# Loading image 0 once: its 32 partitions on ScalarE's queue, the gate's products on them in place

## The chip, the cores and the metric

One core of a Trainium2 chip. The metric is device time in microseconds (us) of one execution; the time before is the median of three runs. Durations below come from one profiled execution of the same program, and times of rows count from the start of its span.

## The reference, cut to what matters

`x` has 32 images of 96 channels, 56 x 56, fp32. Two steps follow each other on it. Cut down:

```python
# step 1: a gate on image 0 picks one of 32 filters for each channel
g    = relu(bn2(einsum('nchw,oc->nohw', x, wg1))).mean(axis=(2, 3))
xg0  = (relu(tanh(g @ wg2.T + bg2)) + beta)[0]
p    = round(xg0[:31] / xg0.sum() * 96)             # the bounds between the filters
filt = ...                                          # (96, 7, 7), chosen by the bounds
xp   = x.reshape(n, 96, 7, 8, 7, 8).mean(axis=(3, 5))
y    = relu(bn1(sum(xp * filt) @ w1d[:, :, 1].T + b1d))
x    = x * (1 + y)
# step 2: a depthwise 3x3 convolution whose taps are made from the image itself
t    = relu(norm(x.mean(axis=(2, 3)) @ w1.T))
wt   = (t @ w2.T + b2) masked to four taps: upper left, up, upper right, left
out  = depthwise_conv(x, wt) + bias
```

Of the gate only image 0 counts, yet the filters of every image hang on it.

## The kernel before, in words

The work is cut into 8 groups of 4 images. A group has 3 tiles of 128 partitions (4 images x 32 rows of channels; channel 3q + t of an image is in tile t), each with 3136 fp32 a partition: 1568 KB. There are 24 tiles, 9 input buffers (`xin`) and 4 output buffers (`xout`). Image 0 is the partitions 0 to 31 of the tiles 0, 1 and 2.

Order of the work: the order in the program of each engine is written by hand, and semaphores join the engines.

- **The gate.** Image 0 is loaded a second time, ahead of the tiles, by three DMAs of 392 KB on SyncE's queue (L338 and L339) into the last output buffer: each row of 3136 pixels is spread as four quarters over four partitions, so that 128 partitions are used. The gate's weights come by a fourfold broadcast (L335) into `gate_one`; VectorE spreads them over a 128 x 128 block `gate_w` (L467), and TensorE makes six matmuls of 128 x 392 (L812), t = 0, 1, 2 by two halves, with two warm products (L779, on zeros) ahead of t = 2. ScalarE takes relu with a sum (L686) and tanh (L689); VectorE and TensorE assign a filter to each channel (L575 to L595), and L833 makes the filters by partition.
- **The cell sums.** Each tile needs its 49 sums of 8 x 8 cells. Tiles 0 to 2 are summed by TensorE (L786, with an identity matrix), VectorE (L504) and GpSimd (L406 folds, VectorE then reduces, L519). Later tiles are folded by GpSimd and reduced by VectorE ahead of their turn: `AHEAD` is 5, and the fold of tile k + 6 stands in GpSimd's program after the edge columns of tile k (L447). The sums of tile 3 (L504 again) stand between the steps that make the coefficients of group 0, and the sum of tile 4 stands in tile 0's turn, after its first tap (L637).
- **The coefficients.** L541 weighs the cells of a group, small matmuls (L841 to L862) with ScalarE and VectorE between them make four taps for each channel and image, and L571 writes them into `coef`.
- **The convolution.** For each tile the output rows are shared: the first 15 by VectorE (L637), 27 by TensorE with VectorE finishing (L871, L647), 14 by TensorE with ScalarE finishing (L880, L738). TensorE uses diagonal matrices of 64 x 64 made by ScalarE (L711); ScalarE seeds banks (L715). L871 works on own rows into own columns, L880 on own rows into the other half's columns.
- **Queues.** SyncE's program issues, in this order: the gate's weights, identity (L337), image 0, the tiles 0, 1, 2 (tile 2 in two parts), the wide constants (L359), tiles 3 to 8, and then, as buffers come free, the load of tile k + 9 (L366 to L368) and the store of tile k (L375). The last tiles' stores are partly crossed (L352): two stores of 64 partitions each. ScalarE's queue carries two small loads: early (the other gate and normalization constants, L679) and narrow (L680).

Of the kernel before, what the change touches and what calls it, by code (L numbers as in the profile page):

```python
# [6 lines left out]
NIMG, C, H, W = 32, 96, 56, 56  # L7
HW = H * W
P = 128
QUAD = 32  # L10
PER = C // QUAD
GROUP = P // QUAD
# [3 lines left out]
BLK = H // DCT  # L16
CELLS = DCT * DCT
NF = 32
# [6 lines left out]
PAD = W  # L25
BANK = 512

IN_BUFS = 9
OUT_BUFS = 4
# [18 lines left out]
QUARTER = HW // 4  # L48
# [5 lines left out]
HEAD_PART = 5  # L54
# [4 lines left out]
E_GATE2 = E_GATE1 + NF  # L59
# [3 lines left out]
E_END = E_HID + 4  # L63
# [11 lines left out]

W_QUARTER = 0
W_IDENT = W_QUARTER + GROUP
W_BIAS = W_IDENT + P
# [48 lines left out]
def build(nc, x, early, narrow, wide, out):  # L127
    fp32 = mybir.dt.float32
    ALU = mybir.AluOpType
# [3 lines left out]
    x_tiles = x.rearrange("n c h w -> (n c) (h w)").rearrange("(g p t) f -> g t p f", p=P, t=PER)  # L133
    out_tiles = out.rearrange("n c h w -> (n c) (h w)").rearrange("(g p t) f -> g t p f", p=P, t=PER)
    x_image0 = x[0, :, :, :].rearrange("c h w -> c (h w)").rearrange("(q t) (j f) -> t q j f", t=PER, j=GROUP)

    with ExitStack() as ctx:
        def sb(name, shape):
            return ctx.enter_context(nc.sbuf_tensor(name, shape, fp32))

        def sem(name):
            return ctx.enter_context(nc.semaphore(name))


        xin = sb("xin", [P, IN_BUFS, PAD + HW])
        xout = sb("xout", [P, OUT_BUFS, HW])
        halves = sb("halves", [P, 2, DCT, BLK * W // 2])
        gate_one = sb("gate_one", [P, PER * E_END])
        gate_w = sb("gate_w", [P, PER, P])
        gate_in = sb("gate_in", [P, E_HID - E_GATE2])  # L150
# [49 lines left out]
        w_hid = wide_sb[0:C, W_HIDE:W_IMAGE]  # L200
        quarter_of = wide_sb[:, W_QUARTER:W_IDENT]
        ident = wide_sb[:, W_IDENT:W_BIAS]
# [3 lines left out]
        to_rows = wide_sb[0:C, W_SPREAD:W_EYE].rearrange("p (t r) -> p t r", t=PER)  # L206
        image0 = xout[:, OUT_BUFS - 1, 0:PER * QUARTER].rearrange("p (t f) -> p t f", t=PER)

# [69 lines left out]
        zeroed = sem("zeroed")  # L278
        gate_placed = sem("gate_placed")
        pad_zeroed = sem("pad_zeroed")  # L280
# [53 lines left out]
        def _(sp):  # L334
            sp.dma_start(gate_one[:, :], early.rearrange("(q j t) e -> q j (t e)", j=1, t=PER).broadcast_to(  # L335
                [QUAD, GROUP, PER * E_END])).then_inc(gate_one_in, 16)
            sp.dma_start(wide_sb[:, 0:W_BIAS], wide[:, 0:W_BIAS]).then_inc(ident_in, 16)  # L337
            for t in range(PER):  # L338
                sp.dma_start(image0[:, t, :], x_image0[t]).then_inc(image0_in[t], 16)  # L339

            def load(k, first=0, end=H):
                return sp.dma_start(xin[:, k % IN_BUFS, PAD + first * W:PAD + end * W],
                                    x_tiles[k // PER, k % PER][:, first * W:end * W])

# [9 lines left out]

            load(0).then_inc(loaded[0], 16)
            load(1).then_inc(loaded[1], 16)
            load(2, 0, HEAD_PART * BLK).then_inc(part_in, 16)
            load(2, HEAD_PART * BLK, H).then_inc(loaded[2], 16)
            sp.dma_start(wide_sb[:, W_BIAS:W_END], wide[:, W_BIAS:W_END]).then_inc(wide_in, 16)  # L359
# [34 lines left out]
        def _(pool):  # L394
# [18 lines left out]

            for j in range(2):
                pool.wait_ge(loaded[j], 16)
                fold_once(j, *FOLDED)
# [5 lines left out]
            def diagonals(k):  # L422
# [6 lines left out]
                                  each.broadcast_to([P, TAPS, HALF]), ALU.mult).then_inc(tail_diag_done, 1)  # L429

            for k in range(TILES):
                if k + 1 < TILES and crossed(k + 1):
# [26 lines left out]
        def _(dve):  # L459
            vec = nc.vector  # L460
            vec.memset(zeros[:, :], 0.0).then_inc(zeroed, 1)
            vec.memset(xin[:, :, 0:PAD], 0.0).then_inc(pad_zeroed, 1)

            dve.wait_ge(gate_one_in, 16)
            dve.wait_ge(ident_in, 16)
            for t in range(PER):
                vec.tensor_tensor(gate_w[:, t, :].rearrange("p (j o) -> p j o", j=GROUP),  # L467
                                  gate_one[:, E_END * t:E_END * t + NF].rearrange("p (j o) -> p j o", j=1).broadcast_to(
                                      [P, GROUP, NF]),
                                  quarter_of.rearrange("p (j o) -> p j o", o=1).broadcast_to([P, GROUP, NF]),  # L470
                                  ALU.mult).then_inc(gate_placed, 1)

# [35 lines left out]
            def sum_array(j):  # L508

                first, end = ARRAY_CELLS[j]  # L510
                dve.wait_ge(array_cells, j + 1)
                return vec.tensor_reduce(stats[:, 0, j % PER, first * DCT:end * DCT],
                                         array_cells_of(j).rearrange("p (c d) -> p c d", d=BLK),
                                         AX.X, ALU.add)
# [65 lines left out]
            dve.wait_ge(assign, 2)  # L580
            vec.tensor_scalar(count[:, :], share[:, :], ROUND, -ROUND, ALU.add, ALU.add).then_inc(counted, 1)
            dve.wait_ge(loaded[0], 16)
            sum_direct(0, 2, 3)
# [13 lines left out]
            sum_once_folded(0, 1, *FOLDED)  # L597
            sum_array(0).then_inc(cells_done, 1)
            dve.wait_ge(loaded[1], 16)
            sum_direct(1, 2, FOLDED[0])  # L600
            sum_once_folded(1, 2, *FOLDED)
            sum_array(1).then_inc(cells_done, 1)
            dve.wait_ge(part_in, 16)
            sum_direct(2, 2, HEAD_PART)
# [72 lines left out]
        def _(act):  # L677
            sca = nc.scalar
            sca.dma_start(early_sb[:, :], early[:, E_GATE2:E_END]).then_inc(early_in, 16)  # L679
            sca.dma_start(narrow_sb[:, :], narrow).then_inc(narrow_in, 16)  # L680
# [46 lines left out]
            def finish_s(k, c):  # L727
# [9 lines left out]
                for own, other in (HALVES, HALVES[::-1]):  # L737
                    sca.activation(xout[own, k % OUT_BUFS, first * W:end * W], acc_s(c)[other, :], ACT.Identity,  # L738
                                   bias=bias[other, k % PER:k % PER + 1]).then_inc(s_out, 1)

            act.wait_ge(folded, 4)
            lift_relu(0)
# [31 lines left out]
        def _(pe):  # L774
# [28 lines left out]
            warm(1)  # L803
            pe.wait_ge(gate_placed, PER)

            for t in range(PER):
                if t == PER - 1:
                    warm(2)
                pe.wait_ge(image0_in[t], 16)
                for half in range(2):  # L810
                    part = slice(GATE_HALF * half, GATE_HALF * (half + 1))
                    ins = mm(gate_out[:, part], gate_w[:, t, :], image0[:, t, part], start=(t == 0), stop=(t == PER - 1))  # L812
            ins.then_inc(gate_mm, 1)
# [9 lines left out]
            for b in range(2):  # L823
                ins = mm(p_bounds[:, b:b + 1], shift[:, b, :], count[:, :], start=True, stop=True)
            ins.then_inc(bounds_mm, 1)
            pe.wait_ge(loaded[0], 16)
            sum_cells(0, 0, 3)
# [122 lines left out]
def constants():  # L950
# [28 lines left out]
    w = np.zeros((P, W_END), np.float32)  # L979
    w[:, W_QUARTER:W_IDENT] = rows[:, None] % GROUP == np.arange(GROUP)  # L980
    w[:, W_IDENT:W_BIAS] = np.eye(P)
# [47 lines left out]
```

## Time and profile before

| | us |
|---|---|
| median of three runs | 212.09 |
| the runs | 212.86, 212.09, 209.39 |
| the profiled execution | 210.17 |
| its span, first to last instruction | 208.3 |

| engine | busy us | share of the span |
|---|---|---|
| PE | 184.4 | 89% |
| DVE | 167.4 | 80% |
| ACT | 148.2 | 71% |
| POOL | 132.4 | 64% |

The DMA engines moved 79.34 MB in the span, 381 GB/s in the mean. The granted TensorE clock was 0.988 in the mean, and 1.00 in the windows of the head. A share of busy time is a mean over stages with different limits: in this kernel the first 34 us, before the convolution of tile 0, differ from the rest. Engine names in the profile: PE is TensorE (PEld its weight loads), DVE VectorE, ACT ScalarE, POOL GpSimd, SPq and ACTq the issue of a DMA by SyncE and ScalarE.

### The profile page before, as it was taken

The numbers are of one execution on the slowest core, as the hardware profiler recorded it, in microseconds if no ns is written. First come the engines' busy times: TensorE is split into PE (matmuls) and PEld (weight loads), VectorE is DVE, ScalarE is ACT, GpSimd is POOL, SyncE is SP. The second block draws the span as 40 slices with busy tenths as digits, with TensorE's granted clock in tenths as the row PEclk, the third lists the DMA queues.
The fourth block names the chain that finished last, engine by engine and source line by source line (L and its number), as shares of the span: only waits on it lengthen the run. The fifth ranks groups of instructions, "written<-read, shape, count | busy, mean of one in ns | idle before, by whom it ended". The sixth has DMA issues, their size and how long they took to land.

```text
span 208.3 us, 4493 instructions
## 1 busy us (share of the span) xinstructions
PE 184.4 (89%) x1678; PEld 106.4 (51%) x1678; DVE 167.4 (80%) x265; ACT 148.2 (71%) x274; POOL 132.4 (64%) x126
## 2 busy tenths in 40 slices
PE   7899999799889988998989988998899989999930
PEld 3448665356445554645554544554456645666610
DVE  3328789997898789879897889868987999789960
ACT  2021017968997989888998899789979975687710
POOL 0333029999999989977997979796970980134000
PEclk9999999999999999999999999999999999999995
DMA  5999999999999999999999999999999877568897
GB/s 137 365 424 430 424 429 423 429 333 361 422 422 424 431 424 426 425 426 426 429 417 440 425 426 424 427 426 432 431 426 417 345 323 271 219 216 292 281 336 254
DMA packets 9366, 79.34 MB, mean 381 GB/s; under 512 B 1248, under 2 KB 1888, under 8 KB 3328
## 3 DMA queue, kind: packets, MB, share of 16 engines
q1 hardware_dynamic: 9184, 78.95, 93.0%
q8 instruction: 13, 0.21, 0.4%
q10 hardware_dynamic: 160, 0.10, 0.2%
q14 instruction: 9, 0.07, 0.1%
HBM read 40.51 MB, written 38.54 MB: 380 GB/s over the span
## 4 chain that ended last, share of the span: by engine, by line
PE 40%; ACT 22%; issue 18%; DVE 11%; DMA 2%; POOL 2%; SPq 1%; DVEq 1%; ACTq 0%; POOLq 0%
PE banks L871 15%; PE banks L880 11%; ACT banks L715 11%; ACT xout L738 6%; ACT diag L711 6%; DVE xout L637 3%; PE banks L862 3%; DMA xout<-x 2%; PE banks L841 2%; PE banks L812 2%; DVE banks L637 2%; DVE xout L647 2%; PE banks L843 2%; POOL halves L406 2%; DVE stats L519 2%
## 5 line engine op out<-in xcount | busy, mean ns | idle before, releaser
L871 PE MATMUL banks<-xin,diag 64*64 64x495 f32 x576 | 129.4, 583 | 11.1 <-ACT banks L715 11.1
L880 PE MATMUL banks<-xin,diag 64*64 64x385 f32 (+1 forms) x768 | 134.5, 491 | 0.0
L406 POOL TENSOR_TENSOR halves<-xin 128x1568 f32<-128x1568 f32 (+1 forms) x22 | 73.8, 3356 | 27.7 <-DMA xin<-x 19.3
L715 ACT ACTIVATE banks<-xin,wide_sb,coef 128x504 f32<-128x504 f32 x95 | 76.4, 827 | 5.1 <-DVE xout L647 4.1
L880 PEld LDWEIGHTS banks<-xin,diag 64*64 64x64 f32 x768 | 49.7, 132 | 30.0 <-issue 21.5
L637 DVE SCALAR_TENSOR_TENSOR banks<-xin,coef,banks 128x825 f32<-128x825 f32 x48 | 51.7, 1078 | 14.0 <-ACT banks L715 14.0
L647 DVE SCALAR_TENSOR_TENSOR xout<-xin,coef,banks 128x495 f32<-128x495 f32 x72 | 52.2, 725 | 4.5 <-PE banks L871 4.5
L871 PEld LDWEIGHTS banks<-xin,diag 64*64 64x64 f32 x576 | 38.6, 132 | 29.6 <-ACT diag L711 16.9
L738 ACT ACTIVATE xout<-banks,wide_sb 64x392 f32<-64x392 f32 x72 | 41.9, 582 | 9.5 <-PE banks L880 8.0
L411 POOL TENSOR_TENSOR halves<-halves 128x784 f32<-128x784 f32 x18 | 33.3, 1849 | 1.4
L637 DVE SCALAR_TENSOR_TENSOR xout<-xin,coef,banks 128x825 f32<-128x825 f32 x24 | 25.6, 1068 | 0.0
L711 ACT ACTIVATE diag<-wide_sb,coef 128x64 f32<-128x64 f32 x72 | 19.2, 335 | 3.0 <-DVE coef L571 2.8
L525 DVE TENSOR_REDUCE stats<-halves 128x49 f32<-128x784 f32 x18 | 17.4, 964 | 0.0
L428 POOL TENSOR_TENSOR diag<-wide_sb,coef 128x256 f32<-128x256 f32 x6 | 3.7, 618 | 20.9 <-DVE coef L571 15.9
L734 ACT ACTIVATE xout<-banks,wide_sb 128x392 f32<-128x392 f32 x12 | 6.9, 577 | 4.4 <-PE banks L880 4.4
L504 DVE TENSOR_REDUCE stats<-xin 128x14 f32<-128x896 f32 (+2 forms) x8 | 8.5, 1075 | 1.1 <-DMA xin<-x 1.1
L855 PEld LDWEIGHTS banks<-hidden,narrow_sb 32*96 32x96 f32 x64 | 6.0, 159 | 5.7 <-ACT hidden L706 5.7
L442 POOL TENSOR_TENSOR edges<-xin,coef 128x84 f32<-128x84 f32 x24 | 8.2, 342 | 0.0
L862 PEld LDWEIGHTS banks<-taps,wide_sb 96*128 96x128 f32 x48 | 6.0, 190 | 4.2 <-issue 4.2
L841 PEld LDWEIGHTS banks<-by_image,wide_sb 128*96 128x96 f32 x48 | 4.7, 164 | 6.3 <-issue 3.7
L445 POOL TENSOR_TENSOR edges<-edges 128x42 f32<-128x42 f32 x24 | 6.6, 275 | 1.9
L447 POOL TENSOR_TENSOR xout<-edges,wide_sb 128x42 f32<-128x42 f32 x24 | 6.4, 268 | 1.9
(80 smaller groups left out, 114.2 us busy)
## 6 DMA issues: line engine op xcount, KB each, us to landing
xin<-x SPq DMA_DIRECT2D x23, 1568.0 KB, 12.8
out<-xout SPq DMA_DIRECT2D x18, 1568.0 KB, 13.7
out<-xout SPq DMA_DIRECT2D x5, 1176.0 KB, 4.5
out<-xout SPq DMA_DIRECT2D x10, 196.0 KB, 5.1
xout<-x SPq DMA_DIRECT2D x3, 392.0 KB, 4.7
xin<-x SPq DMA_DIRECT2D x1, 1120.0 KB, 14.9
out<-xout SPq DMA_DIRECT2D x1, 924.0 KB, 4.2
wide_sb<-wide SPq DMA_DIRECT2D x1, 467.5 KB, 15.9
```

Source lines behind the costliest of these rows:

```text
L406: eng.tensor_tensor(halves[:, j % 2, first:end, :], cells[:, :, 0, :], cells[:, :, 1, :], ALU.add).then_inc(once_folded, 1)
L411: eng.tensor_tensor(cells[:, :, 0, :], cells[:, :, 0, :], cells[:, :, 1, :], ALU.add).then_inc(twice_folded, 1)
L525: return vec.tensor_reduce(cells_of(j), halves[:, j % 2, :, 0:2 * W].rearrange("p a (b c d) -> p a c b d", c=DCT, d=BLK), AX.XY, ALU.add)
L637: return vec.scalar_tensor_tensor(out=to, in0=grid(k)[:, irows, cols], scalar=weight(k, which), in1=acc, op0=ALU.mult, op1=ALU.add)
L647: vec.scalar_tensor_tensor(out=result(k)[:, first:end, ocols], in0=grid(k)[:, irows, cols], scalar=weight(k, LEFT), in1=acc_b(c).rearrange ...
L711: sca.activation(diag[:, k % 2, which, :], eye, ACT.Copy, scale=weight(k, which)).then_inc(diag_done, 1)
L715: return sca.activation(acc, above_rows(k, first, end), ACT.Identity, bias=bias[:, k % PER:k % PER + 1], scale=weight(k, UP))
L738: sca.activation(xout[own, k % OUT_BUFS, first * W:end * W], acc_s(c)[other, :], ACT.Identity, bias=bias[other, k % PER:k % PER + 1]).then ...
L841: mm(p_mixed, w_mix[:, t, :], by_image[:, 1, t, :], start=(t == 0), stop=(t == PER - 1))
L862: ins = mm(p_spread[:, TAPS * t:TAPS * (t + 1), :], to_rows[:, t, :], taps[:, :, :], start=True, stop=True)
L871: ins = mm(to[own], diag[own, k % 2, which, :], grid(k)[own, irows, cols], start=False, stop=(which == RIGHT_UP), skip_group_check=True)
L880: ins = mm(to[other], diag[own, k % 2, which, :], grid(k)[own, irows, cols], start=(which == UP), stop=(which == LEFT), skip_group_check=True)
```

## The change

Image 0 is no longer loaded a second time. SyncE loads the partitions 32 to 127 of the tiles 0, 1 and 2; the partitions 0 to 31 come by three DMAs of 392 KB on ScalarE's queue, into the same buffers. The gate's products read them there: for each quarter of the pixels one matmul of 32 rows and 32 columns, into another 32 partitions of the same banks, with the gate's weights as they were loaded. The spread weights, the broadcast and the column block that it needed are gone. Whoever reads a tile 0, 1 or 2 first waits for both loads. SyncE's first issue is now tile 0; identity comes behind it.

```diff
 @block.sync
-            sp.dma_start(gate_one[:, :], early.rearrange("(q j t) e -> q j (t e)", j=1, t=PER).broadcast_to(
-                [QUAD, GROUP, PER * E_END])).then_inc(gate_one_in, 16)
-            sp.dma_start(wide_sb[:, 0:W_BIAS], wide[:, 0:W_BIAS]).then_inc(ident_in, 16)
-            for t in range(PER):
-                sp.dma_start(image0[:, t, :], x_image0[t]).then_inc(image0_in[t], 16)
-            load(0).then_inc(loaded[0], 16)
-            load(1).then_inc(loaded[1], 16)
-            load(2, 0, HEAD_PART * BLK).then_inc(part_in, 16)
-            load(2, HEAD_PART * BLK, H).then_inc(loaded[2], 16)
+            others = slice(QUAD, P)
+            load(0, parts=others).then_inc(loaded[0], 16)
+            sp.dma_start(wide_sb[:, 0:W_BIAS], wide[:, 0:W_BIAS]).then_inc(ident_in, 16)
+            load(1, parts=others).then_inc(loaded[1], 16)
+            load(2, 0, HEAD_PART * BLK, others).then_inc(part_in, 16)
+            load(2, HEAD_PART * BLK, H, others).then_inc(loaded[2], 16)
 @block.gpsimd
             for j in range(2):
+                pool.wait_ge(image0_in[j], 16)
                 pool.wait_ge(loaded[j], 16)
                 fold_once(j, *FOLDED)
...
+            pool.wait_ge(image0_in[2], 16)
             for k in range(TILES):
 @block.vector
-            dve.wait_ge(gate_one_in, 16)
-            dve.wait_ge(ident_in, 16)
-            for t in range(PER):
-                vec.tensor_tensor(gate_w[:, t, :].rearrange("p (j o) -> p j o", j=GROUP),
...
-                                  ALU.mult).then_inc(gate_placed, 1)
...
+            dve.wait_ge(image0_in[0], 16)
             dve.wait_ge(loaded[0], 16)
             sum_direct(0, 2, 3)
...
+            dve.wait_ge(image0_in[1], 16)
             dve.wait_ge(loaded[1], 16)
...
+            dve.wait_ge(image0_in[2], 16)
             dve.wait_ge(part_in, 16)
 @block.scalar
-            sca.dma_start(early_sb[:, :], early[:, E_GATE2:E_END]).then_inc(early_in, 16)
+            sca.dma_start(gate_one[:, :], early.rearrange("(q t) e -> q (t e)", t=PER)).then_inc(gate_one_in, 16)
+            for t in range(PER):
+                sca.dma_start(xin[0:QUAD, t, PAD:], x_tiles[0, t][0:QUAD, :]).then_inc(image0_in[t], 16)
+                if t == 0:
+                    sca.dma_start(early_sb[:, :], early[:, E_GATE2:E_END]).then_inc(early_in, 16)
             sca.dma_start(narrow_sb[:, :], narrow).then_inc(narrow_in, 16)
...
+            for t in range(PER):
+                act.wait_ge(image0_in[t], 16)
             act.wait_ge(folded, 4)
             lift_relu(0)
 @block.tensor
-            pe.wait_ge(gate_placed, PER)
+            pe.wait_ge(gate_one_in, 16)
             for t in range(PER):
                 if t == PER - 1:
                     warm(2)
                 pe.wait_ge(image0_in[t], 16)
                 for half in range(2):
                     part = slice(GATE_HALF * half, GATE_HALF * (half + 1))
-                    ins = mm(gate_out[:, part], gate_w[:, t, :], image0[:, t, part], start=(t == 0), stop=(t == PER - 1))
+                    for j in range(GROUP):
+                        pixels = slice(PAD + QUARTER * j + part.start, PAD + QUARTER * j + part.stop)
+                        ins = mm(gate_out[QUAD * j:QUAD * (j + 1), part], gate_one[:, E_END * t:E_END * t + NF],
+                                 xin[0:QUAD, t, pixels], start=(t == 0), stop=(t == PER - 1))
...
             ins.then_inc(bounds_mm, 1)
+            pe.wait_ge(ident_in, 16)
             pe.wait_ge(loaded[0], 16)
```

`load` has a further argument for the partitions; `gate_one` has 32 partitions; `gate_w`, `image0` and the columns `W_QUARTER` of the wide constants are gone.

## Rows read from the trace of the kernel before

**Rows 1.** The page's second part: busy tenths of the DMA engines in 40 slices

```profile
DMA  5999999999999999999999999999999877568897
```

**Rows 2.** Waits, whole span: waiter, releaser, us in total, times, longest

```profile
POOL halves L406 <- DMA xin<-x: 19.3, 4, 10.9
...
DVE stats L504 <- DMA xin<-x: 1.1, 1, 1.1
...
PE banks L812 <- DMA xout<-x: 0.7, 1, 0.7
```

**Rows 3.** DMA issues of the page: count, KB each, median us to landing

```profile
xin<-x SPq DMA_DIRECT2D x23, 1568.0 KB, 12.8
```

**Rows 4.** Timeline, POOL, 97 to 120: start, us, engine, line, what, count

```profile
97.36 0.27 POOL L447 TENSOR_TENSOR xout<-edges,wide_sb 128x42 f32<-128x42 f32 x1
...
119.34 0.27 POOL L447 TENSOR_TENSOR xout<-edges,wide_sb 128x42 f32<-128x42 f32 x1
```

**Rows 5.** The chain that ended last, 0 to 34: start, us, what

```profile
2.09 4.37 DMA xout<-x
...
9.47 1.32 PE banks L779 x4
10.79 1.31 PE banks L812 x4
...
18.28 0.79 PE banks L833 x6
...
30.06 3.53 POOL halves L406
...
33.61 1.79 DVE stats L519
```

**Rows 6.** Timeline, 0 to 34, and SyncE's crossed stores near 180

```profile
0.73 0.39 ACTq L679 DMA_DIRECT2D early_sb<-early  x1
...
4.01 2.54 SPq L342 DMA_DIRECT2D xin<-x  x4
...
7.15 0.16 DVE L485 TENSOR_TENSOR b_gate<-gate_in,b_gate 128x1 f32<-128x1 f32 x1
...
13.82 1.61 POOL L406 TENSOR_TENSOR halves<-xin 128x672 f32<-128x672 f32 x1 [6.07 <-DMA xin<-x]
...
17.58 1.60 POOL L406 TENSOR_TENSOR halves<-xin 128x672 f32<-128x672 f32 x1 [2.16 <-DMA xin<-x]
...
24.12 0.31 DVE L541 TENSOR_TENSOR stats<-stats,banks 128x147 f32<-128x147 f32 x1
...
26.23 1.55 DVE L504 TENSOR_REDUCE stats<-xin 128x21 f32<-128x1344 f32 x1 [1.09 <-DMA xin<-x]
...
30.96 0.20 DVE L571 TENSOR_REDUCE coef<-spread 128x12 f32<-128x48 f32 x1
...
32.39 1.08 DVE L637 SCALAR_TENSOR_TENSOR banks<-xin,coef,banks 128x825 f32<-128x825 f32 x1
...
179.63 1.92 SPq L352 DMA_DIRECT2D out<-xout  x2
```

**Rows 7.** Windows of 1 us: busy by engine, then granted clock, DMA share, GB/s

```profile
1.00:2.00 1.00, 0.55 (x1) 0.50 (x2) 0.87 (x2) 0.38 (x1) 0.00 (x0) 1.00 0.11 15
...
8.00:9.00 1.00, 1.00 (x5) 0.58 (x4) 0.57 (x7) 0.00 (x0) 0.00 (x0) 1.00 0.97 392
...
183.00:184.00 1.00, 1.00 (x16) 0.63 (x12) 1.00 (x2) 0.78 (x1) 0.00 (x0) 1.00 0.96 211
```

**Rows 8.** Landing times of L679 (early), then of L339 (image 0), by line

```profile
DMA to landing us min/median/max: 1.8/1.8/1.8
...
DMA to landing us min/median/max: 4.4/4.7/6.6
```

**Rows 9.** Timeline, PE and its weight loads, 111.4 to 111.5

```profile
111.40 0.63 PE L871 MATMUL banks<-xin,diag 64*64 64x495 f32 x2
111.42 0.54 PE L880 MATMUL banks<-xin,diag 64*64 64x385 f32 x2
...
111.47 0.14 PEld L880 LDWEIGHTS banks<-xin,diag 64*64 64x64 f32 x2
```

More of the change, by code:

```diff
@@ L73 @@
 N_END = N_TAP + TAPS * C
-W_QUARTER = 0
-W_IDENT = W_QUARTER + GROUP
+W_IDENT = 0
 W_BIAS = W_IDENT + P
@@ L134, in build @@
     out_tiles = out.rearrange("n c h w -> (n c) (h w)").rearrange("(g p t) f -> g t p f", p=P, t=PER)
-    x_image0 = x[0, :, :, :].rearrange("c h w -> c (h w)").rearrange("(q t) (j f) -> t q j f", t=PER, j=GROUP)
     with ExitStack() as ctx:
@@ L147, in build @@
         halves = sb("halves", [P, 2, DCT, BLK * W // 2])
-        gate_one = sb("gate_one", [P, PER * E_END])
-        gate_w = sb("gate_w", [P, PER, P])
+        gate_one = sb("gate_one", [QUAD, PER * E_END])
         gate_in = sb("gate_in", [P, E_HID - E_GATE2])
@@ L200, in build @@
         w_hid = wide_sb[0:C, W_HIDE:W_IMAGE]
-        quarter_of = wide_sb[:, W_QUARTER:W_IDENT]
         ident = wide_sb[:, W_IDENT:W_BIAS]
@@ L206, in build @@
         to_rows = wide_sb[0:C, W_SPREAD:W_EYE].rearrange("p (t r) -> p t r", t=PER)
-        image0 = xout[:, OUT_BUFS - 1, 0:PER * QUARTER].rearrange("p (t f) -> p t f", t=PER)
         banks = ctx.enter_context(nc.psum_tensor("banks", [P, 8, BANK], fp32))
@@ L278, in build @@
         zeroed = sem("zeroed")
-        gate_placed = sem("gate_placed")
         pad_zeroed = sem("pad_zeroed")
@@ L334, in _, with load @@
         def _(sp):
-            sp.dma_start(gate_one[:, :], early.rearrange("(q j t) e -> q j (t e)", j=1, t=PER).broadcast_to(
-                [QUAD, GROUP, PER * E_END])).then_inc(gate_one_in, 16)
-            sp.dma_start(wide_sb[:, 0:W_BIAS], wide[:, 0:W_BIAS]).then_inc(ident_in, 16)
-            for t in range(PER):
-                sp.dma_start(image0[:, t, :], x_image0[t]).then_inc(image0_in[t], 16)
-            def load(k, first=0, end=H):
-                return sp.dma_start(xin[:, k % IN_BUFS, PAD + first * W:PAD + end * W],
-                                    x_tiles[k // PER, k % PER][:, first * W:end * W])
+            def load(k, first=0, end=H, parts=slice(0, P)):
+                return sp.dma_start(xin[parts, k % IN_BUFS, PAD + first * W:PAD + end * W],
+                                    x_tiles[k // PER, k % PER][parts, first * W:end * W])
+            others = slice(QUAD, P)
             def store(k, first=0, end=H):
@@ L462, in _ @@
             vec.memset(xin[:, :, 0:PAD], 0.0).then_inc(pad_zeroed, 1)
-            dve.wait_ge(gate_one_in, 16)
-            dve.wait_ge(ident_in, 16)
-            for t in range(PER):
-                vec.tensor_tensor(gate_w[:, t, :].rearrange("p (j o) -> p j o", j=GROUP),
-                                  gate_one[:, E_END * t:E_END * t + NF].rearrange("p (j o) -> p j o", j=1).broadcast_to(
-                                      [P, GROUP, NF]),
-                                  quarter_of.rearrange("p (j o) -> p j o", o=1).broadcast_to([P, GROUP, NF]),
-                                  ALU.mult).then_inc(gate_placed, 1)
             dve.wait_ge(early_in, 16)
@@ L979, in constants @@
     w = np.zeros((P, W_END), np.float32)
-    w[:, W_QUARTER:W_IDENT] = rows[:, None] % GROUP == np.arange(GROUP)
     w[:, W_IDENT:W_BIAS] = np.eye(P)
```

## The prediction

> **What bounds the kernel now.** I read the page's 40 slices first: the DMA engines are at nine tenths or more from the second slice to the thirtieth [rows 1]. That looks like a kernel bound by bytes, and the change takes 1.2 MB of some 79 MB away. The waits of the whole span say otherwise: POOL's fold at L406 is held by a landing four times, 19.3 us together, and DVE and PE lose 1.1 and 0.7 us [rows 2]; the starts of these waits in the timeline all lie before 34 us. After that no engine waits for a load worth naming. The loads have room: a tile lands 12.8 us after its issue [rows 3], while POOL folds it some three tiles after the buffer came free, and three tiles take 119.34 - 97.36 = 22.0 us [rows 4]. So from about 34 us the tiles go at the pace of PE, ACT and DVE, and the end moves only as far as the start of tile 0 moves.
>
> The chain of the head shows what sets that start [rows 5]. There are two ropes. **The computing rope**: the gate's product ends at 10.79 + 1.31 = 12.10 us; relu, tanh, the assignment and the filter follow, L833 ends at 19.07, the array sums and the direct sums of tiles 1 and 2 come next, DVE weighs the cells at 24.12, then stands 1.09 us for tile 3, and the coefficients are done at 30.96 + 0.20 = 31.16 [rows 6]. From 12.10 to 24.12 PE or DVE is at work nearly all the time and no landing holds them, so I treat these 12.0 us as fixed: the coefficients come 31.16 - 12.10 - 1.09 = 18.0 us after the gate once tile 3 is early. **The DMA rope**: tile 4 lands, POOL folds it from 30.06 for 3.53 us, and DVE's sum of it begins at 33.61 [rows 5]. DVE itself reaches that instruction at 32.39 + 1.08 = 33.47 [rows 6], so both ropes end together, and the gain is the smaller of their two gains.
>
> **The change part by part.**
>
> *Bytes and queues.* Three loads of 392 KB and the fourfold copy of the gate's weights go. Instead ACT issues a 30 KB load, three loads of 392 KB into 32 partitions, early and narrow: six issues at 0.39 us or a little more (early's row [rows 6]), some 2.7 us in place of 0.8. ACT's table load and first Tanh move from 1.6 to about 3.5 us and stay hidden, as ACT next waits for the gate. SP no longer spends its first 3.2 us on other issues: tile 0 was issued at 4.01, and now goes first, at about 0.7 [rows 6].
>
> *How fast the two queues move.* Bytes start at about 2.0 us (15 GB/s in the second microsecond [rows 7]) for an issue at 0.73; early lands 1.8 us after its issue [rows 8], so some 0.5 us follow the last byte. ACT's first image load starts one issue later, 2.4 us. I let the two queues share alike, so that ACT's 1.20 MB go beside 1.20 MB of SP's: 2.41 MB. The pace is the open number. Upper end: a whole tile every 17.58 - 13.82 = 3.76 us [rows 6], 427 GB/s. Lower end: the only narrow transfers of this trace, the last tiles' crossed stores of 64 partitions, move 211 GB/s while the DMA engines are 0.96 busy, in the microsecond from 183 (a pair was issued from 179.63 on, behind that tile's wide store [rows 6]); the loads of image 0 and of tile 0 together, full width, made 392 at 0.97 [rows 7]. The mean of the ends is 319, the mixed row is 392; I take 350, between these two.
>
> The Trainium skill has a rule that speaks against this change ("SBUF — State Buffer", Door 1: The DMA port swizzle): 32 or 64 partitions from 0 on reach only 8 of 16 ports, so width is lost. The crossed stores agree, 211 against 427 GB/s. By the page's 218 GB/s for eight ports, 64 of SP's 96 partitions would crowd on the other eight; the first three tiles take 11.0 us if the queues interleave well and 16.6 us if they take turns, an estimate of about 302 GB/s, by which the gate would end at 12.4 us and the gain be 0.8 us.
>
> *The gate.* At 350 GB/s the three image loads land at 2.4 + 2.3 + 0.5 = 5.2, 7.5 and 9.8 us (now: the first 4.4, the last 6.6 us after its issue, at 6.5 and about 10.0 [rows 5, 8]). A step t cost PE 1.31 us as four passes of 128x392 [rows 5]. It becomes eight matmuls, sixteen passes, on four column groups of the same 32 rows. If the groups run side by side, a step still costs 1.31, plus about 0.15 for the wait and the change of shape. For that speaks that the L871 and L880 matmuls, which read the same 64 rows into different columns, start 0.02 us apart, two of each [rows 9]. So step 1 ends at 8.95, the two warm products before step 2 take 1.32 [rows 5] to 10.27, step 2 then has its load and ends at 11.73. The gate is 0.4 us earlier than 12.10. At the upper end (427) the loads land at 6.7 and 8.5 and the gate ends at 10.9; at 319, 12.1; at 211 the last load lands at 14.3 and the gate ends at 15.7.
>
> The Trainium skill states that a weight load overlaps a running matmul only where the row group differs ("TensorE: Matmul & The Clock Gate", Part 3). Here all four groups have the same rows; 16 loads of 0.14 us would add some 2.2 us a step, and the gate would end near 17 us, the kernel some 4 us later. The trace disagrees: L880's next weight load starts at 111.47, while matmuls begun at 111.40 and 111.42 occupy both row halves.
>
> *What goes from DVE and what waits.* The three products into gate_w go; the gate waited for its image then, not for them, so nothing is saved. Early now lands behind the first image load, about 5.3 us, 2.8 later than the 2.5 of now; the gate's parameters, done at 7.31 now [rows 6], come by 10.1 at the latest, ahead of the gate's 11.73. Narrow lands behind image load 2, about 10.3, and is wanted only after the gate. The new waits for image loads 0 to 2 stand in front of POOL's folds (behind them its folds of tiles 4 and 5), DVE's sums (behind them the weighing) and ACT's first relu of the loop (behind it every seed). All of these come after 13 us and the loads are in by 10, so each costs nothing unless the narrow pace rules. The identity matrix now comes behind tile 0 and is wanted after the assignment's count, later than the gate.
>
> *The DMA rope.* Up to tile 2 there are now 4.82 MB of tiles and 0.20 MB of constants: at 350 GB/s, 14.3 us, landing at 16.8. Then 0.48 MB of wide constants (1.1 us) and tiles 3 and 4 (3.76 each): tile 4 at 25.4 instead of 30.06, 4.6 us earlier. At 427 it is 22.9, at 211 throughout 34.9.
>
> **Sum.** DMA rope: 4.6 earlier. Computing rope: 0.4 from the gate and 1.09 of waiting for tile 3, 1.5 earlier. The smaller counts. The profiled execution's 210.17 us (span 208.3, 1.9 around it) would become 208.7; the median of the runs shown, 212.09, lies 1.9 above the profiled one, and from it I forecast 210.6 us. With paces from 319 to 427 the gain is 1.1 to 2.3 us: 209.8 to 211.0.
>
> **The rivals.**
>
> *ACT's loads run ahead of SP's* (0.15). If they get the full pace, image 2 lands at 2.4 + 2.8 + 0.5 = 5.7, and PE's order sets the gate: 3.8 + 4 x 1.32, 9.1 us. Gain 3.0 + 1.09 = 4.1, which the DMA rope just allows: 208.0 us. Against it: nothing in this trace gives ACT's queue a preference over SP's.
>
> *Nothing is left* (0.22). If the gate ends at 13.2 us, from a pace of some 280 GB/s or a slower change of shape on PE, its delay eats the 1.09 us: 212.1 us, and the bytes saved are hidden, since the steady tiles never waited for them.
>
> *The narrow pace rules the head* (0.13, the slower side). Engines serve both queues, so 32-partition and 96-partition pieces could hold each other at the 211 GB/s of the crossed stores until tile 2. Tile 4 lands at 34.9, POOL's fold of it ends at 38.4 instead of 33.6: 4.8 us later, 216.9 us; it decides as soon as tile 4 lands after 30.06, a mean pace under 265 GB/s. For it: the one narrow row. Against it: those stores ran alone, and here the other partitions' load runs beside.
>
> *The column groups run one after another* (0.06). Sixteen passes of 0.33 us are 5.2 us a step: 5.2 + 3 x 5.2 + 1.3 = 22.1 us for the gate, 10.0 late, less 1.09: some 221 us. Rows 9 speak against it, for two column groups at least.
>
> That the image is loaded once but the time does not follow bytes is contained in the second rival.
>
> **How the numbers follow.** The forecast has 0.44. What a measurement of this kernel can tell from no change is about 2%, 4.2 us. Faster by that needs the first rival and a little more: 0.14 with the spread of the runs (209.39 to 212.86). Slower by that are the third and fourth rival for the most part, 0.16. The rest is 0.70. The range goes from 207.7, below the first rival, to 215.5, into the third.
>
> **What would show it.** Right: gate matmuls with starts 0.02 us apart in fours and a step of about 1.4 us; the last image landing before 10.5; POOL's fold of tile 4 beginning near 25 and no DVE wait for tile 3; coefficients near 29.7; the spacing of later tiles unchanged. Wrong: steps of 3 us or more; DMA share near one at 200 to 300 GB/s between 3 and 15 us; a fold of tile 4 after 30; or a later stage that starts to wait for loads or stores.

## The result, and the profile after

| | before | after |
|---|---|---|
| median, same chip, four runs each (us) | 210.88 | 221.67 |
| lowest to highest (us) | 209.39 to 212.86 | 218.59 to 222.89 |
| ratio, 95% interval | | 1.0517 [1.0454, 1.0581] |
| profiled execution, span (us) | 210.17, 208.3 | 221.61, 219.8 |

The change costs 10.8 us; 210.6 was forecast, and 221.67 lies outside the range. The ratios here and below leave disturbed runs out and the medians don't, so a ratio is not always the quotient of the two medians.

In the new kernel L668 is the issue of an image load, L807 the gate's product, L772 the warm products, L525 the weighing and L555 the coefficients (before: L339, L812, L779, L541, L571). First the page's 40 slices of the kernel after, 5.5 us each (of before: [rows 1]):

```profile
PEclk9855699999999999999999999999999999999995
DMA  7999999940999999999999999999999986578887
GB/s 190 223 242 244 397 431 423 425 185 0 292 422 390 420 428 422 425 425 436 416 427 433 422 431 421 431 429 428 425 431 421 422 351 262 191 266 291 295 308 279
```

The DMA digits of the head look as they did: nines. The GB/s line under them doesn't: the first four slices move 190 to 244 where the next two move 397 and 431. Windows of the same kernel show where that ends, with the granted clock before the DMA share (compare [rows 7]):

```profile
3.00:4.00 1.00, 1.00 (x2) 0.33 (x1) 0.00 (x0) 0.17 (x1) 0.00 (x0) 1.00 0.99 348
...
9.00:10.00 1.00, 0.00 (x0) 0.00 (x0) 0.00 (x0) 0.00 (x0) 0.00 (x0) 0.50 1.05 216
...
23.00:24.00 1.00, 1.00 (x6) 0.51 (x3) 0.00 (x0) 0.62 (x1) 0.00 (x0) 0.50 1.13 439
...
26.00:27.00 1.00, 1.00 (x5) 0.43 (x4) 0.20 (x1) 0.25 (x1) 0.00 (x0) 0.99 0.97 414
4.00:23.00 19.00, 13.22 (x56) 3.67 (x54) 4.35 (x18) 1.32 (x2) 4.74 (x5) 0.63 1.01 238
```

The last of these windows in the kernel before:

```profile
4.00:23.00 19.00, 18.17 (x93) 12.04 (x92) 10.21 (x38) 2.05 (x5) 4.79 (x5) 1.00 0.99 402
```

Two things go wrong together. The DMA engines are full at 238 GB/s as a mean from 4 to 23 us, against 402 in the same window of before; and TensorE, idle from 6.1 to 10.3 us, has a granted clock of 0.50, its 1.2 GHz level, from 9 to 26 us, where the head of before was at 1.00. The timeline of the head shows what both do (compare [rows 6]):

```profile
5.03 1.08 PE L772 MATMUL banks<-zeros 128*128 128x392 f32 x2
10.33 2.84 PE L807 MATMUL banks<-xin,gate_one 32*32 32x392 f32 x16 [4.22 <-DMA xin<-x]
...
14.73 2.83 PE L807 MATMUL banks<-xin,gate_one 32*32 32x392 f32 x16 [1.56 <-DMA xin<-x]
17.50 2.98 PE L772 MATMUL banks<-zeros 128*128 128x392 f32 x4
...
20.41 2.84 PE L807 MATMUL banks<-xin,gate_one 32*32 32x392 f32 x16
...
34.23 6.98 POOL L397 TENSOR_TENSOR halves<-xin 128x1568 f32<-128x1568 f32 x2 [13.32 <-DVE stats L496]
36.86 0.31 DVE L525 TENSOR_TENSOR stats<-stats,banks 128x147 f32<-128x147 f32 x1
37.79 1.55 DVE L488 TENSOR_REDUCE stats<-xin 128x21 f32<-128x1344 f32 x1
...
43.14 0.20 DVE L555 TENSOR_REDUCE coef<-spread 128x12 f32<-128x48 f32 x1
```

The gate's three steps take 2.84 us each and end at 23.25 instead of 12.10. The weighing comes at 36.86 instead of 24.12, the coefficients at 43.34 instead of 31.16: 12.2 us, and the span is 11.5 longer. Three tiles still take 22.0 us afterwards (L440's rows of POOL at 95.34 and 117.37). So the whole loss is made in the head, and 11.15 us of it before the gate ends. The chain of the head says the same (compare [rows 5]):

```profile
2.13 12.56 DMA xin<-x
...
17.57 2.91 PE banks L772 x4
20.48 2.77 PE banks L807 x16
23.25 2.91 PE banks L772 x4
```

The three image loads landed 9.0, 12.6 and 15.6 us after their issue, at 10.2, 14.7 and 18.3; the view of their line has

```profile
DMA to landing us min/median/max: 9.0/12.6/15.6
```

where [rows 8] had 4.4 to 6.6. The waits of the first 60 us (compare [rows 2]):

```profile
POOL halves L397 <- DVE stats L496: 13.3, 1, 13.3
...
DVE gate_in L459 <- DMA early_sb<-early: 8.6, 1, 8.6
...
PE banks L807 <- DMA xin<-x: 5.8, 2, 4.2
...
POOL halves L397 <- DMA xin<-x: 4.4, 1, 4.4
```

POOL's fold of tile 4, held by its load before, now waits for VectorE, which is late because of the gate. Tile 4 itself landed 28.0 us after its issue near 4.4, at about 32.4, before POOL came to it at 34.23. The DMA rope has become slack, although its loads are slower; the computing rope is the end.

### The profile page after: what moved, and what is told of

It reads as the page before. It is cut to its first block, busy times and chain, and to the rows that moved or that the text cites. A ratio compares the mean times of both kernels' runs of the same rounds, so it can differ in the third digit from the quotient of the medians.

```text
span 219.8 us, 4569 instructions
## 1 busy us (share of the span) xinstructions
PE 192.0 (87%) x1714; PEld 106.9 (49%) x1714; DVE 168.9 (77%) x262; ACT 148.2 (67%) x274; POOL 132.6 (60%) x126
## 3 DMA queue, kind: packets, MB, share of 16 engines
q10 hardware_dynamic: 352, 1.34, 2.7%
## 4 chain that ended last, share of the span: by engine, by line
PE 43%; ACT 21%; issue 13%; DVE 12%; DMA 6%; ACTq 1%; DVEq 1%
PE banks L868 14%; PE banks L877 11%; ACT banks L706 10%; DMA xin<-x 6%; ACT xout L729 6%; ACT diag L702 5%; PE banks L772 3%; DVE xout L624 3%; PE banks L807 3%; PE banks L859 2%; DVE banks L624 2%; PE banks L779 2%; PE banks L838 2%; PE banks L840 2%; DVE xout L634 2%
## 5 line engine op out<-in xcount | busy, mean ns | idle before, releaser
L868 PE MATMUL banks<-xin,diag 64*64 64x495 f32 x576 | 129.4, 582 | 11.1 <-ACT banks L706 11.1
L420 POOL TENSOR_TENSOR diag<-wide_sb,coef 128x256 f32<-128x256 f32 x6 | 3.7, 619 | 20.9 <-DVE coef L555 16.1
L807 PE MATMUL banks<-xin,gate_one 32*32 32x392 f32 x48 | 8.5, 855 | 5.8 <-DMA xin<-x 5.8
L677 ACT ACTIVATE banks<-banks,b_gate,a_gate 128x784 f32<-128x784 f32 x1 | 1.0, 977 | 18.0 <-PE banks L807 18.0
L772 PE MATMUL banks<-zeros 128*128 128x392 f32 x14 | 8.9, 760 | 0.0
L559 DVE TENSOR_SCALAR xg<-gate_act,gate_in 32x1 f32<-32x1 f32 x1 | 0.2, 201 | 10.8 <-ACT gate_act L680 10.8
## 6 DMA issues: line engine op xcount, KB each, us to landing
xin<-x ACTq DMA_DIRECT2D x3, 392.0 KB, 12.6
```

Source lines behind the costliest of these rows:

```text
L772: mm(banks[:, BANK_D, 0:columns], zeros[:, 0:P], zeros[:, 0:columns], start=True, stop=True)
L807: ins = mm(gate_out[QUAD * j:QUAD * (j + 1), part], gate_one[:, E_END * t:E_END * t + NF], xin[0:QUAD, t, pixels], start=(t == 0), stop=(t ...
L868: ins = mm(to[own], diag[own, k % 2, which, :], grid(k)[own, irows, cols], start=False, stop=(which == RIGHT_UP), skip_group_check=True)
```

## The experiments

Three causes are to be told apart: the **width** of the loads (32 and 96 partitions), the **two queues**, and the **clock**. After that: whether the idea can win at all. In the diffs `...` stands for lines that are left out.

### The clock alone

```diff
-                if t == PER - 1:
-                    warm(2)
+                warm((6, 4, 3)[t])
                 pe.wait_ge(image0_in[t], 16)
```

> The changed kernel with 6, 4 and 3 warm products ahead of the gate's steps 0, 1 and 2 (it has 0, 0, 2), so that PE stands idle less. Theory C (part of the loss is TensorE's clock, granted at 0.50 from 9 to 26 us): granted clock 1.00 through the head, image loads land as before (10.2, 14.7, 18.3 us), a gate step takes 1.4 us instead of 2.8, the gate ends near 19.9 instead of 23.25, the two warm products behind it cost 1.3 instead of 3.0; the coefficients come about 5 us earlier, near 38.3, and the time is about 216.7 us. Theory L (the landings alone set it, the clock is incidental): within 1 us of the changed kernel's 221.7.

217.68 us, ratio 1.0352 [1.0322, 1.0382]. Timeline and window of this kernel:

```profile
10.23 1.52 PE L806 MATMUL banks<-xin,gate_one 32*32 32x392 f32 x16 [0.23 <-DMA xin<-x]
...
19.79 1.52 PE L806 MATMUL banks<-xin,gate_one 32*32 32x392 f32 x16
...
39.81 0.20 DVE L555 TENSOR_REDUCE coef<-spread 128x12 f32<-128x48 f32 x1
```

```profile
4.00:23.00 19.00, 17.18 (x85) 7.52 (x83) 4.36 (x18) 2.58 (x4) 4.75 (x5) 1.00 1.00 229
```

With warm products in the gaps the clock stays at 1.00 and a step takes 1.52 us instead of 2.84; the loads move at 229 GB/s, as slowly as in the change. The clock is therefore worth 3.3 us of the coefficients (43.34 to 40.01) and, by the ratios, 1.65% or 3.5 us. That is less than the 5 us foretold: the second and third image load landed later still, 14.0 and 16.1 us after their issue. The rest lies with the loads: how fast they move, and in which order.

### Width or two queues

**One queue, same widths.** The three loads of 32 partitions go first on SyncE's queue, then the ones of 96; ScalarE's queue keeps the small loads:

```diff
+            for t in range(PER):
+                sp.dma_start(xin[0:QUAD, t, PAD:], x_tiles[0, t][0:QUAD, :]).then_inc(image0_in[t], 16)
             load(0, parts=others).then_inc(loaded[0], 16)
...
-            for t in range(PER):
-                sca.dma_start(xin[0:QUAD, t, PAD:], x_tiles[0, t][0:QUAD, :]).then_inc(image0_in[t], 16)
```

> The changed kernel with the three loads of image 0 (32 partitions) on SyncE's queue, ahead of the tiles' 96 partitions; ScalarE's queue has only the small loads. Theory N (pieces that do not span 128 partitions move at about half pace, whatever the queue): 200 to 250 GB/s up to tile 2, image loads land near 4.5, 6.5 and 8.3 us, tile 2 still near 21 to 23 us. Theory Q (two queues with large loads hinder each other): 400 GB/s or more from 3 us, image load 2 lands by 6 us and tile 2 by 15 us.

216.32 us (four runs from 213.11 to 219.87), ratio 1.0164 [1.0115, 1.0213]. Windows of a run of 218.51 us: first the loads of 32 partitions, with 0.10 MB of small loads among 1.09 MB, then those of 96, with a few small rows of constants:

```profile
3.00:8.00 5.00, 5.00 (x25) 1.66 (x27) 0.05 (x1) 0.62 (x2) 0.00 (x0) 1.00 1.06 218
...
13.00:22.00 9.00, 9.00 (x32) 3.75 (x25) 1.86 (x8) 1.35 (x3) 3.20 (x2) 0.50 1.00 249
```

In the second window SyncE's queue alone moves data, and the pace stays narrow. It is the width, and a load of 96 partitions is hardly faster than one of 32.

The time says a second thing. From 4 to 23 us these loads move at 237 GB/s, as in the change, yet the kernel is 1.0164 and not 1.0517 of the one before. In front on one queue the image's loads landed 5.0, 6.5 and 8.8 us after their issue instead of 9.0, 12.6 and 15.6, and the gate's last step began at 11.59 instead of 20.41:

```profile
11.59 2.83 PE L806 MATMUL banks<-xin,gate_one 32*32 32x392 f32 x16
...
39.97 0.20 DVE L557 TENSOR_REDUCE coef<-spread 128x12 f32<-128x48 f32 x1
```

So at the same narrow pace the order in which the bytes land decides most of the loss. In this run the clock stood at 0.50 from 10 to 30 us, though PE's busy share was 1.00 in every microsecond from 2 us on: a wait of TensorE is not the only thing that can stand ahead of a fall of the clock.

**Two queues, full width.** The kernel before with image 0's spread loads (128 partitions) on ScalarE's queue:

```diff
-            for t in range(PER):
-                sp.dma_start(image0[:, t, :], x_image0[t]).then_inc(image0_in[t], 16)
...
+            for t in range(PER):
+                sca.dma_start(image0[:, t, :], x_image0[t]).then_inc(image0_in[t], 16)
```

> The kernel before with its three loads of image 0 (spread over 128 partitions) on ScalarE's queue, so that SyncE's queue begins with the tiles, whole. Two queues, both wide. Theory N: the pace is that of the kernel before, 370 to 430 GB/s from 4 us on, image load 2 lands near 9 to 10 us, tile 4 is folded from about 29 to 30 us; time within 1.5 us of the kernel before. Theory Q: 200 to 250 GB/s while ScalarE's queue has image loads, image load 2 lands at 12 us or later, the time 2 to 6 us above the kernel before.

214.83 us, ratio 1.0233 [1.0183, 1.0282]. A window, then the queues from 2 to 16 us (packets, MB, share of the engines):

```profile
4.00:23.00 19.00, 14.34 (x46) 7.04 (x45) 5.43 (x31) 2.77 (x5) 4.78 (x5) 0.91 1.02 392
```

```profile
q1 hardware_dynamic: 608, 3.71, 68.2%
q10 hardware_dynamic: 583, 1.30, 31.1%
```

392 GB/s against 402: two queues of full width cost little pace. What they do is share the engines. The packets are 608 to 583, nearly one for one, and the bytes 3.71 to 1.30 MB, as a spread row of image 0 is 3,136 bytes and a tile's row 12,544. So the image's three loads, in front by their issue, landed only 3.6, 9.0 and 13.6 us after it, and the gate was late once more: its last step began at 16.33 instead of 10.62. The clock fell here too, to 0.91 in the mean of the window.

**Halves.** Perhaps partitions 0 to 63 and 64 to 127, on two queues, fill each other's gaps (the added warm products are not shown):

```diff
-            others = slice(QUAD, P)
+            others = slice(2 * QUAD, P)
...
-                sca.dma_start(xin[0:QUAD, t, PAD:], x_tiles[0, t][0:QUAD, :]).then_inc(image0_in[t], 16)
+                sca.dma_start(xin[0:2 * QUAD, t, PAD:], x_tiles[0, t][0:2 * QUAD, :]).then_inc(image0_in[t], 16)
```

> The changed kernel with the split at partition 64: ScalarE's queue loads partitions 0 to 63 of tiles 0 to 2, SyncE's 64 to 127 (and 3, 2, 2 warm products ahead of the gate's steps). Theory P (the lower and the upper 64 partitions have different paths, and two queues that each use one fill both): 400 GB/s or more up to tile 2. Theory W (any piece narrower than 128 partitions moves at half pace, and two of them share that): 200 to 250 GB/s, tile 2 complete past 20 us.

and the same two halves behind each other on SyncE's queue:

> The same split at partition 64, both halves on SyncE's queue, the lower half of a tile first (no image loads on ScalarE's; 3 warm products ahead of steps 1 and 2). Theories P and W alike: 200 to 250 GB/s, as one half follows the other, unless the DMA engines run so far apart that halves overlap (up to 330).

One run each: 223.41 and 222.06 us. The window of the first, then of the second:

```profile
4.00:23.00 19.00, 13.36 (x48) 4.78 (x47) 4.36 (x18) 1.49 (x2) 4.75 (x5) 0.70 0.99 226
```

```profile
4.00:23.00 19.00, 13.54 (x60) 4.93 (x62) 2.23 (x18) 0.00 (x0) 4.77 (x5) 0.82 1.01 222
```

226 on two queues, 222 on one: complementary halves don't add up.

**Narrow beside whole.** The image on ScalarE's queue into spare output buffers, 32 partitions, where the gate reads it, with whole tiles on SyncE's and warm products ahead of the steps (the loads alone are shown):

```diff
-            others = slice(QUAD, P)
+            others = slice(0, P)
...
-                sca.dma_start(xin[0:QUAD, t, PAD:], x_tiles[0, t][0:QUAD, :]).then_inc(image0_in[t], 16)
+                sca.dma_start(xout[0:QUAD, 1 + t, :], x_tiles[0, t][0:QUAD, :]).then_inc(image0_in[t], 16)
```

> The changed kernel with image 0 loaded twice again: three loads of 32 partitions on ScalarE's queue into output buffers, where the gate reads them, and tiles 0 to 2 whole on SyncE's queue (warm products 6, 4, 3). Tells whether a narrow load drags a whole one along. If it does: 200 to 270 GB/s while ScalarE's queue has image loads, then 420. If only the narrow pieces themselves are slow: 350 GB/s or more in the sum. Image load 2 past 14 us in the first case, by 11 us in the second.

216.94 us, one run.

```profile
6.00:14.00 8.00, 8.00 (x36) 3.85 (x36) 2.84 (x9) 0.00 (x0) 2.50 (x4) 1.00 1.00 252
...
16.00:24.00 8.00, 8.00 (x46) 3.70 (x43) 1.55 (x7) 1.35 (x3) 1.60 (x1) 1.00 1.01 416
```

While narrow loads are in the queue even a whole tile beside them goes at 252 in the sum; once they are through, 416. A narrow load costs its neighbours their pace too.

### Whole tiles, the gate in place

The part of the idea that is free of narrow loads: SyncE loads whole tiles, and the gate reads the 32 partitions where they lie.

```diff
-            load(0, parts=others).then_inc(loaded[0], 16)
+            load(0).then_inc(loaded[0], 16)
...
-                if t == PER - 1:
-                    warm(2)
-                pe.wait_ge(image0_in[t], 16)
+                if t > 0:
+                    warm(3)
+                pe.wait_ge(loaded[t], 16)
```

> The changed kernel with tiles 0 to 2 loaded whole, 128 partitions, on SyncE's queue; the gate reads image 0 in place and waits for the whole tile; three warm products ahead of steps 1 and 2. Theory N: 420 GB/s or more from 3 us on, tiles land near 6.5, 10.3 and 14.2 us, the gate ends near 15.7, the coefficients come near 33.7 and the time is some 2.5 us above the kernel before, 213 to 214 us. Theory G (reading image 0 in place by four column groups is itself slow): a gate step of 2.8 us or more even at full clock, and the gate's end past 17.

216.94 us, ratio 1.0338 [1.0292, 1.0383]: the pace is wide (418 GB/s from 4 to 23 us), but TensorE stood idle before the first step, and that step and the warm products after it ran at half speed. So once more, with `warm((2, 3, 3)[t])`:

> e3 (tiles 0 to 2 whole on SyncE's queue, the gate in place) with two warm products more ahead of the gate's step 0, as e3's matmuls ran at half rate from 7.9 to 14 us after 1.4 us of idle PE. Theory N+C (width sets the pace, the clock the rest): steps of 1.5 us throughout, gate's end near 17.2 instead of 19.8, coefficients near 35.8 instead of 38.5, time near 214.3. If the clock does not fall for the idle time: gate's end past 19 again, time 216 to 217.

214.37 us, ratio 1.0197 [1.0132, 1.0263]. Timeline:

```profile
8.26 1.52 PE L795 MATMUL banks<-xin,gate_one 32*32 32x392 f32 x16
...
12.13 1.52 PE L795 MATMUL banks<-xin,gate_one 32*32 32x392 f32 x16 [0.18 <-DMA xin<-x]
...
15.98 1.52 PE L795 MATMUL banks<-xin,gate_one 32*32 32x392 f32 x16 [0.16 <-DMA xin<-x]
...
36.01 0.20 DVE L550 TENSOR_REDUCE coef<-spread 128x12 f32<-128x48 f32 x1
```

With clock and pace both restored the coefficients are still 5.0 us later than before. Each step now waits for a whole tile, 3.8 us apart, and the last one ends at 17.50, 5.4 us after the 12.10 of before. The second copy of image 0 bought exactly that: the gate's data ahead of the tiles.

### The cell sums ahead of the gate's chain

While the gate waits for tiles 1 and 2, the cell sums of the tiles already there can be made; before, they stood behind the gate. A first version put the identity matrix on ScalarE's queue:

> Tiles 0 to 2 whole on SyncE's queue and the gate in place, as in e3, but each tile's array sums (TensorE) and direct sums (VectorE) stand right behind its landing instead of behind the gate's chain, the identity matrix comes on ScalarE's queue, the first array's bank and the warm products' bank are moved for that. Theory: with full-width loads the pace is 400 GB/s or more, tile 2 lands near 15.3, the gate ends near 17, its chain without the sums in it takes some 7 us to the weighing (12 in the kernel before), coefficients near 30 against 31.2; the time is 1 to 2 us below the kernel before. If the chain is bound elsewhere (waits of PE behind sums, a lower clock): coefficients at 32 or later and no gain.

A miss: 223.5 us, six runs from 212.99 to 224.76. In this kernel the warm products run over a bank that had been prepared for the convolution's first rows, so a part of these isn't added up. In the profiled run of 224.76 us the identity landed 11.1 us after its issue (from 1.65 to 12.73) beside the whole tiles, TensorE stood 2.3 us for it, and the second and third step took 2.84 us. The next version issues early first and the identity behind tile 0, both on SyncE's queue, and opens all three banks behind the sums; what each part is worth was not tried. Its diff against the whole tiles with warm products:

```diff
+            sp.dma_start(early_sb[:, :], early[:, E_GATE2:E_END]).then_inc(early_in, 16)
             load(0).then_inc(loaded[0], 16)
             sp.dma_start(wide_sb[:, 0:W_BIAS], wide[:, 0:W_BIAS]).then_inc(ident_in, 16)
...
+            dve.wait_ge(loaded[0], 16)
+            sum_direct(0, 2, 4)
...
+                if t < 2:
+                    pe.wait_ge(ident_in, 16)
+                    sum_cells(t, 0, BLK)
             ins.then_inc(gate_mm, 1)
-            warm(2)
+            sum_cells(2, 0, 5)
```

> e5's order (the sums of tiles 0 to 2 behind their landings, ahead of the gate's chain), with early first on SyncE's queue, identity behind tile 0, only the gate's weights and narrow on ScalarE's, and the three banks primed after the sums. Theory: tiles land near 8.2, 12.0 and 15.8 us at 410 GB/s or more, clock 1.00 as PE has sums between the gate's steps, gate's end near 17.5, weighing near 24.5, coefficients near 30.5 against 31.2, time 0.5 to 1.5 us below the kernel before. If the parts in between wait on each other (identity, POOL's folds beside VectorE): coefficients past 33, no gain.

210.34 us, ratio 0.9994 [0.9965, 1.0024]. Timeline:

```profile
24.10 2.84 PE L773 MATMUL banks<-zeros 128*128 128x512 f32 x6
...
25.32 0.18 DVE L527 TENSOR_TENSOR by_image<-sums,banks 128x24 f32<-128x24 f32 x1
...
26.78 0.59 PE L827 MATMUL banks<-by_image,wide_sb 128*96 128x4 f32 x6
...
31.85 0.20 DVE L551 TENSOR_REDUCE coef<-spread 128x12 f32<-128x48 f32 x1
```

The sums by image are ready at 25.50; the mix (L827) waits until 26.78, as three opening products (L773) stand in front of it. Two of these can take the place of warm products inside the gate's chain:

```diff
             ins.then_inc(bounds_mm, 1)
-            warm(1)
+            prime(BANK_B + 1)
...
-            warm(1)
+            prime(BANK_B)
...
-            prime(BANK_B)
-            prime(BANK_B + 1)
             pe.wait_ge(cells_done, 1)
             prime(BANK_B + 2)
```

> Differs from the run with the sums ahead (whole tiles 0 to 2 on SyncE, gate in place, sums of tiles 0 to 2 ahead of the gate's chain) only in where the three opening products over banks stand: two of them take the place of warm products that were there anyway in the gate's chain, one stays ahead of the mix. There the three began at 24.10 us and the mix at 26.78 us, though the sums by image were ready at 25.50 us. If those products set the mix's start: mix at about 25.6 us, coefficients ready at 30.7 to 31.0 us in place of 32.05, time 209.1 us (208.8 to 209.6), that is 0.995 of the kernel before. If the coefficients are not what sets the end any more, and POOL's fold of tile 4 (25.61 us) or the loads are: coefficients earlier and time still 210.3 us.

209.28 us, ratio 0.9971 [0.9936, 1.0005]. Timeline:

```profile
25.66 0.64 PE L827 MATMUL banks<-by_image,wide_sb 128*96 128x4 f32 x6 [0.41 <-DVE by_image L527]
...
25.85 3.50 POOL L395 TENSOR_TENSOR halves<-xin 128x1568 f32<-128x1568 f32 x1 [12.33 <-DMA xin<-x]
...
30.77 0.20 DVE L551 TENSOR_REDUCE coef<-spread 128x12 f32<-128x48 f32 x1
```

Mix and coefficients came where foretold, 1.1 us earlier, and the profiled span went from 208.6 to 207.5. The two kernels ran on different chips, each beside the kernel before; by the ratios the step is 0.23%, some 0.5 us, and the intervals overlap. Against the kernel before the interval touches one: loading image 0 once can be had for nothing, together with the moved sums and opening products, with at most a small gain. Whether the kernel before would gain from the same moves with its second copy kept, no run shows.

| kernel | ratio to before | coefficients at (us) | GB/s, 4 to 23 us |
|---|---|---|---|
| before | 1 | 31.16 | 402 |
| the change | 1.0517 | 43.34 | 238 |
| image first on one queue, same widths (clock at 0.50) | 1.0164 | 40.17 | 237 |
| the change, clock kept | 1.0352 | 40.01 | 229 |
| and whole tiles | 1.0197 | 36.21 | 416 |
| and sums ahead | 0.9994 | 32.05 | 422 |
| and opening products moved | 0.9971 | 30.97 | 423 |

## Why the prediction was wrong

- **What bounds the kernel: right.** Time follows the start of tile 0 (coefficients 12.2 us later, span 11.5), and the tiles' spacing stayed at 22.0 us for three.
- **The landing of the image: the step that failed, in two terms.** The first is the pace: "I take 350, between these two." It was 238. The nearest row for a narrow transfer was the crossed stores' 211 GB/s at a DMA share of 0.96 [rows 7]; I set it aside because "those stores ran alone". The share in that row speaks against this: engines that are full at 211 leave no room for a neighbour, and the narrow loads beside whole tiles made 252 in the sum. The 392 that I leaned on came from loads of full width. The Trainium skill goes beyond the rule that I cited: "SBUF — State Buffer", section "Can I just issue two DMAs to hit both halves?", says that the swizzle looks at one transfer's partitions and can't fuse two, so only one transfer over all 128 reaches all the ports. The halves' 226 GB/s agree, as do the 218 of the 32-partition loads, which is that page's figure for eight ports; the 249 of 96 partitions lies above it. The recorded estimate by that page, 302 GB/s and a gain of 0.8 us, was too fast as well.
- **The second term: the share of the queues.** "I let the two queues share alike" from 2.4 us. They did not:

```profile
q1 hardware_dynamic: 402, 2.74, 64.6%
q10 hardware_dynamic: 350, 1.34, 34.6%
```

  This is the queue view of the kernel after from 2 to 19 us: SyncE's queue moved 2.74 MB and ScalarE's 1.34, of the latter only 0.03 until 5 us. The packets are near one for one again, but only 96 of ScalarE's 350 are rows of the image (1.20 MB at 12,544 bytes); the others belong to its small loads. That these cost the image its turns is argued from the counts, no run moved them alone. By the prediction's own sum at 238 GB/s the last image lands at 13.0 and the gate ends at 14.5, 2.4 us late. It landed at 18.3, 5.3 us later still; the remaining 3.5 of the gate's 11.15 us are steps and warm products at half clock. The kernel with the image first on one queue bears this out: the same pace, and 1.0164.
- **The clock: not in the sum.** The step was priced at 1.31 us plus 0.15 from rows at a granted clock of 1.00. At full clock it takes 1.52 us, close to that; in the change it took 2.84, at a clock of 0.50 that followed TensorE's wait for the late image. The warm products show what this was worth, some 3.5 us of the time, and none of my cases had it.
- **Column groups: right.** Sixteen passes in 1.52 us at full clock are four groups side by side, and the serial rival's 5.2 us is false. The Trainium skill's rule on weight loads ("TensorE: Matmul & The Clock Gate", Part 3) would have added 2.2 us a step; no run here shows that, and the steps of 1.52 us hold sixteen weight loads each.
- **18.0 us after the gate: 2.1 short.** 43.34 - 23.25 = 20.1. Up to the weighing it was 13.6 instead of 12.0, some 1.5 of it the warm pair after the gate, 2.98 us at half clock instead of 1.48. The wait of 1.09 us for tile 3 went, as foretold, but only 0.56 came off between weighing and coefficients (6.48 for 7.04).
- **The DMA rope: no longer bound.** Tile 4's fold waited for VectorE, not for its load, which had come at about 32.4 instead of the 25.4 forecast.
- **The nearest rival** was the narrow pace, at 0.13. Its pace was near (211 for 238), its path was not: it let tile 4's landing decide, 4.8 us late, with the gate's end at 15.7. Tile 4 came in time, and the gate ended at 23.25, through the share and the clock. That even whole tiles at the wide pace cost 4.1 us (1.0197) was in no case either: the prediction noted when the spread copy lands, and did not ask what its place ahead of all tiles was worth.

## What to carry to other kernels

Look at the number of partitions that a transfer spans before its bytes: loads of 32, 64 or 96 partitions kept the DMA engines full at 218 to 252 GB/s here, whole tiles beside them included. Then ask in which order the bytes of a serial chain land. The narrow pace alone, with the image in front, cost 1.6%; with the image behind a share of the queues and the clock gone, the same pace cost 5.2%. A second copy of a small piece can be what lets a serial chain start early; price it by when its data land, against the landing of what would replace it. Where a wait grows in front of TensorE, price the work behind it at half clock as well.

## What the runs showed that I had not expected

- The granted clock of the record can stand at 1.00 while matmuls run at half speed. In the kernel with whole tiles and fewer warm products, timeline and window:

```profile
7.91 2.83 PE L796 MATMUL banks<-xin,gate_one 32*32 32x392 f32 x16 [1.37 <-DMA xin<-x]
...
14.70 1.52 PE L796 MATMUL banks<-xin,gate_one 32*32 32x392 f32 x16
```

```profile
8.00:9.00 1.00, 1.00 (x8) 0.32 (x12) 0.88 (x7) 0.00 (x0) 0.00 (x0) 1.00 0.98 414
```

  The same sixteen passes, 2.83 and 1.52 us: the duration tells it, the clock column doesn't.

- Small loads pay for large neighbours: early, which took 1.8 us in the kernel before [rows 8], came 8.8 us after its issue in the change (at 10.5), and the identity 11.1 us after it in the first version with sums ahead.
- VectorE's products for `b_gate`, 128 x 1, take 0.16 us, as the one at 7.15 [rows 6]. In the change one of them (L467) took 2.38 us from 12.53 on, and POOL's fold ran from 13.30 to 14.88 beside it, ending 0.03 us before it did. No run here tells why.
